# Windowed attention on one core: scores in four row groups of three heads, one division per image, values made per 128 tokens

## What is computed

```python
x = x.transpose(0, 2, 3, 1)                      # 32, 16, 16, 96
xs = roll(layernorm(x), (-4, -4))
xw = windows of 8x8 tokens                       # 128 windows, 64 tokens, 96
q, k, v = (xw @ qkv_w + qkv_b)                   # 12 heads of 8 channels; q * 8**-0.5
attn = softmax(q @ k.T + bias + mask)            # 64x64 per window and head
out = (attn @ v) @ proj_w + proj_b
x = shortcut + roll(windows back, (4, 4))
x = x + mlp(layernorm(x))
```

## Time and profile before

| | us |
|---|---|
| median of 3 runs | 540.69 |
| range of the runs | 535.23 to 543.65 |
| span of the profiled execution | 540.4 |
| TensorE busy | 518.1 (96%) |
| VectorE busy | 365.9 (68%) |
| ScalarE busy | 302.1 (56%) |
| GpSimd busy | 178.3 (33%) |

### The profile page before, as it was taken

The page is one execution under the profiler, slowest core; times in us unless marked ns, Lnnn a source line. Parts: engine busy times, 40 slices in busy tenths (PEclk is TensorE's granted clock), DMA queues, the critical chain, the costliest instruction groups (busy, mean ns, idle before and its releaser), DMA issues. The chain is left out here.

```text
span 540.4 us, 23612 instructions
## 1 busy us (share of the span) xinstructions
PE 518.1 (96%) x9134; PEld 343.1 (63%) x9134; DVE 365.9 (68%) x1003; ACT 302.1 (56%) x763; POOL 178.3 (33%) x216
## 2 busy tenths in 40 slices
PE   7999999999999999998899999939999999999996
PEld 6777777777777777776674343339655655555553
DVE  1479999999999999997404354436556565656544
ACT  2278877777787778876435563103444444444432
POOL 8433444444434443344200220022433332333300
PEclk8599999999999999999999999957999999999999
DMA  4111111111111101100130132323454434444411
GB/s 83 29 42 32 30 30 46 29 30 30 30 29 24 26 24 29 29 3 2 45 75 21 46 93 71 88 49 79 121 146 124 115 101 118 121 114 105 117 51 32
DMA packets 41177, 32.51 MB, mean 60 GB/s; under 512 B 19240, under 2 KB 36776, under 8 KB 41128
## 3 DMA queue, kind: packets, MB, share of 16 engines
q1 hardware_dynamic: 37544, 26.11, 18.9%
q0 software_dynamic: 3584, 5.72, 4.8%
HBM read 18.36 MB, written 7.13 MB: 47 GB/s over the span
## 5 line engine op out<-in xcount | busy, mean ns | idle before, releaser
L383 POOL TENSOR_TENSOR scores<-scores,peak 128x768 f32<-128x768 f32 x64 | 94.3, 1473 | 135.3 <-DVE peak L552 135.3
L1224 POOL DMA_DIRECT2D x_stack<-padded_x x96 | 52.4, 548 | 97.4 <-PE ps_v L1497 63.4
L446 ACT COPY probs_t<-ps_probs 128x768 f32<-128x768 f32 x64 | 51.1, 799 | 40.7 <-PE ps_probs L706 40.7
L544 DVE TENSOR_TENSOR scores<-ps_scores,bias 128x768 f32<-128x768 f32 x64 | 61.3, 957 | 9.1 <-PE ps_scores L696 7.4
L552 DVE TENSOR_REDUCE peak<-scores 128x12 f32<-128x768 f32 x64 | 61.0, 953 | 2.4
L719 PE MATMUL ps_out<-v_blocks,probs_t 128*64 128x54 f32 x1536 | 57.2, 224 | 1.0 <-ACT out_t L451 0.9
L719 PEld LDWEIGHTS ps_out<-v_blocks,probs_t 128*64 128x64 f32 x1536 | 50.2, 138 | 12.3 <-issue 12.2
L706 PE MATMUL ps_probs<-ident,scores 128*128 128x128 f32 x384 | 55.0, 279 | 0.0
L440 ACT ACTIVATE scores<-scores 128x768 f32<-128x768 f32 x64 | 54.2, 846 | 0.6 <-POOL scores L383 0.6
L1037 ACT ACTIVATE hidden<-ps_hidden,fc_b_folded 128x512 f32<-128x512 f32 x48 | 29.1, 688 | 36.8 <-PE ps_hidden L978 36.8
L1497 PE MATMUL ps_qk<-x_stack,conv_w 40*32 40x256 f32 x1536 | 48.8, 379 | 0.0
(11 more groups left out here) (156 smaller groups left out, 900.2 us busy)
## 6 DMA issues: line engine op xcount, KB each, us to landing
x_stack<-padded_x SPq DMA_DIRECT2D x96, 54.0 KB
x_stack<-padded_x POOLq DMA_DIRECT2D x96, 54.0 KB, 2.7
padded_x<-x_pad SPq DMA_DIRECT2D x32, 121.5 KB, 2.5
x_sliced<-stream SPq DMA_DIRECT2D x48, 64.0 KB, 2.0
mixed<-y_sliced SPq DMA_DIRECT2D x48, 64.0 KB, 2.0
out<-y_sb SPq DMA_DIRECT2D x32, 96.0 KB, 2.0
x_now<-in_x SPq DMA_DIRECT2D x32, 72.0 KB, 1.8
stream<-in_x SPq DMA_DIRECT2D x32, 72.0 KB, 1.9
```

Source lines behind the costliest of these rows:

```text
L383: nc.gpsimd.tensor_tensor(sc, sc, peak[:, par, p, :].unsqueeze(2).to_broadcast((128, HEADS, WN)), ALU.subtract).then_inc(s["shifted"], 1)
L446: nc.scalar.copy(probs_t[:, :], ps_turned).then_inc(s["turned_copied"], 1)
L544: nc.vector.tensor_tensor(scores[:, par, p, :].rearrange("p (g c) -> p g c", g=NG), ps_scores[:, :, 0:GROUP * WN], bias[:, p, :].rearrange ...
L1224: engine.dma_start(x_stack[64 * half + i * HC:64 * half + (i + 1) * HC, slot, :, :], rows).then_inc(landed[slot], 16)
```

## The change

The 12 heads are put in four row groups of three heads (24 channels, padded to 32) instead of three groups of four: the weights of queries and keys become 128 columns wide, the key copies three instead of four. Values of 128 tokens are made by one product with all 96 columns; ScalarE then moves each window's even and odd heads to the partition half where `weigh` wants them, four copies instead of two. `weigh` uses 32 columns of weights and 18 columns of values a product, four products side by side. Both halves of an image are divided at once, and both are transposed and copied in one go. The bank `ps_b` is gone: values and projection go into the tails of two banks of `ps_scores`, so `score(t, 0)` waits for the copied values and an earlier residual. `copy_v` moves forward in ScalarE's order and `make_v` and `project` move in TensorE's. The offset's folding at the start is made of 22 products (half of them with one row, adding the bias), one load fewer precedes it.

```diff
-NG = HEADS // GROUP
+TRIO = 3
+NG = HEADS // TRIO
+GROUP_C = TRIO * HD
+WIDE = 32 * NG
+PARTS_W = 4
...
-    v_blocks = sb("v_blocks", [128, 2, PAIRS, 2, HP + 2, 2, VC])
+    v_blocks = sb("v_blocks", [128, 2, PAIRS, 2, HP, 2, VC])
...
-    ps_b = bank("ps_b")
...
-    ps_v = ps_b[:, 0, 0:2 * C].rearrange("p (w q d) -> p w q d", w=2 * PAIRS, d=HD)
-    ps_proj = ps_b[0:C, 0, 0:N]
+    ps_q, ps_k = (ps_scores[:, g, N:2 * N] for g in range(2))
+    ps_v = ps_scores[:, 2, TRIO * WN:TRIO * WN + PAIRS * C].rearrange("p (a q e d) -> p a q e d", a=PAIRS, e=2, d=HD)
+    ps_proj = ps_scores[0:C, 3, N:2 * N]
...
             for e in range(2):
-                half = slice(64 * e, 64 * e + 64)
-                nc.scalar.copy(v_blocks[half, par, :, :, 0:HP, e, 0:HD].rearrange("p a b q d -> p (a b) q d"),
-                               ps_v[half]).then_inc(s["v_copied"], 1)
+                for window in range(2):
+                    nc.scalar.copy(v_blocks[64 * e:64 * e + 64, par, :, window, :, e, 0:HD],
+                                   ps_v[64 * window:64 * window + 64, :, :, e, :]).then_inc(s["v_copied"], 1)
...
-        def weigh_heads(t, p):
...
+        def weigh_heads(t):
+            dve.wait_ge(s["pv_ready"], (t + 1) * 2)
+            need(dve, s["heads_ready"], t)
+            nc.vector.reciprocal(recip[:, :, :], ps_pv[:, :, :, HD]).then_inc(s["recip_ready"], 1)
...
+            for k in range(3):
+                for g in range(NG if k < 2 else SLICES):
+                    at = k * C + g * (GROUP_C if k < 2 else 32)
+                    home = ps_biases[32 * g:32 * g + 32, k:k + 1]
+                    nc.tensor.matmul(home, w_in[:, at:at + 32], cols[:, 1:2], start=True, stop=False, skip_group_check=True)
+                    mm = nc.tensor.matmul(home, b_row[:, at:at + 32], one[:, :], start=False, stop=True, skip_group_check=True)
+                mm.then_inc(pe_set, 1)
...
         def make_v(t):
-            need(pe, s["residual_done"], t - 2)
-            heads = w_qkv[:, 2 * C:3 * C].rearrange("c (q e d) -> c q e d", e=2, d=HD)
-            for window in range(2 * PAIRS):
-                for e in range(2):
-                    mm = nc.tensor.matmul(ps_v[64 * e:64 * e + 64, window, :, :], normed[:, window * WN:(window + 1) * WN],
-                                          heads[:, :, e, :], start=True, stop=True, skip_group_check=True)
+            for p in range(PAIRS):
+                mm = nc.tensor.matmul(ps_v[:, p, :, :, :].rearrange("p q e d -> p (q e d)"), normed[:, p * 2 * WN:(p + 1) * 2 * WN],
+                                      w_qkv[:, 2 * WIDE:2 * WIDE + C], start=True, stop=True, skip_group_check=True)
...
+            if p == 0:
+                pe.wait_ge(s["v_copied"], (t + 1) * 4)
+                need(pe, s["residual_done"], t - 2)
...
-                    mm = nc.tensor.matmul(ps_scores[64 * w:64 * w + 64, g, 0:GROUP * WN], q, k, start=True, stop=True,
+                    mm = nc.tensor.matmul(ps_scores[64 * w:64 * w + 64, g, 0:TRIO * WN], q, k, start=True, stop=True,
...
-            pe.wait_ge(s["v_copied"], (t + 1) * 2)
-            need(pe, s["ot_copied"], u)
+            if p == 0:
+                need(pe, s["ot_copied"], t * PAIRS)
             pe.wait_ge(s["turned_copied"], u + 1)
             for q in range(HP):
-                for top in range(2):
-                    mm = nc.tensor.matmul(ps_out[64 * top:64 * top + 64, 0, q * 2 * VC:(q + 3) * 2 * VC],
-                                          probs_t[:, q * 128 + 64 * top:q * 128 + 64 * top + 64],
-                                          v_blocks[:, par, p, top, q:q + 3, :, :].rearrange("p q e c -> p (q e c)"),
+                for part in range(PARTS_W):
+                    at = q * 128 + 32 * part
+                    mm = nc.tensor.matmul(ps_pv[32 * part:32 * part + 32, p, 2 * q:2 * q + 2, :],
+                                          probs_t[:, at:at + 32], v_blocks[:, par, p, part // 2, q, :, :],
```

More of the change, by code:

```diff
@@ L217, in window_attention @@
     w_in = sb("w_in", [C, 3 * C])
-    w_qkv = sb("w_qkv", [C, 3 * C])
+    w_qkv = sb("w_qkv", [C, 2 * WIDE + C])
     w_proj = sb("w_proj", [C, C])
     cols = sb("cols", [C, 6])
-    b_q = sb("b_q", [C, 1])
-    b_k = sb("b_k", [C, 1])
+    b_row = sb("b_row", [1, 3 * C])
+    one = sb("one", [1, 1])
+    b_q = sb("b_q", [WIDE, 1])
+    b_k = sb("b_k", [WIDE, 1])
     b_v = sb("b_v", [C, 1])
@@ L254, in window_attention @@
     ps_folded = ps_scores[0:C, 2, 0:3 * C]
[L255 to L257 removed]
+    ps_q, ps_k = (ps_scores[:, g, N:2 * N] for g in range(2))
+    ps_v = ps_scores[:, 2, TRIO * WN:TRIO * WN + PAIRS * C].rearrange("p (a q e d) -> p a q e d", a=PAIRS, e=2, d=HD)
+    ps_proj = ps_scores[0:C, 3, N:2 * N]
     ps_turned = ps_probs.rearrange("p b c -> p (b c)")[:, 0:SC]
[L259 to L260 removed]
+    ps_pv = ps_out[:, 0, 0:PAIRS * HEADS * VC].rearrange("p (a h c) -> p a h c", h=HEADS, c=VC)
+    ps_ot = ps_out[0:C, 0, N:2 * N].rearrange("p (a n) -> p a n", a=PAIRS)
+    ps_biases = ps_out[:, 0, 0:3]
+    ps_b_proj = ps_out[0:C, 0, 3:4]
     first_homes = [ps_scores[:, 0, :], ps_scores[:, 1, :], ps_scores[:, 2, :], ps_a[:, 0, :]]
@@ L303, in _ @@
                  (cols[:, 0:1], column("L0_conv_norm1_g")), (cols[:, 1:2], column("L0_conv_norm1_b")),
-                 *((cols[:, 2 + k:3 + k], a["L0_conv_qkv_b"][k * C:(k + 1) * C].rearrange("(c a) -> c a", a=1))
-                   for k in range(3)),
-                 (head_mask[:, :], a["c_head_mask"]))
+                 (b_row[:, :], a["L0_conv_qkv_b"].rearrange("(a c) -> a c", a=1)),
+                 (head_mask[0:C, :], a["c_head_mask"][:, 0:TRIO]), (head_mask[C:WIDE, :], a["c_head_mask"][0:32, 0:TRIO]))
         second = (*((shift_mask[WN * top:WN * (top + 1), left, :], a["c_shift_mask"][WN * left:WN * (left + 1), top])
@@ L353, in _ @@
     def _(pool):
+        nc.gpsimd.memset(one[:, :], 1.0).then_inc(one_set, 1)
         nc.gpsimd.memset(eps[:, :], EPS).then_inc(zeroed, 1)
@@ L508, in set_up_projection @@
             dve.wait_ge(pe_set, 4)
-            nc.vector.tensor_tensor(b_proj[:, :], ps_out[0:C, 0, 0:1], cols[:, 5:6], ALU.add).then_inc(set_up, 1)
+            nc.vector.tensor_tensor(b_proj[:, :], ps_b_proj, cols[:, 5:6], ALU.add).then_inc(set_up, 1)
         def measure(t):
@@ L645, in fold_v @@
             pe.wait_ge(set_up, 4)
-            nc.tensor.matmul(ps_out[0:C, 0, 0:1], w_proj[:, :], b_v[:, 0:1], start=True, stop=True).then_inc(pe_set, 1)
+            nc.tensor.matmul(ps_b_proj, w_proj[:, :], b_v[:, 0:1], start=True, stop=True,
+                             skip_group_check=True).then_inc(pe_set, 1)
         def fold_mean():
@@ L781, in step @@
                 weigh(t, 1, par)
+            if real(t + 2):
+                make_v(t + 2)
+            if real(t - 1):
+                project(t - 1, 1 - par)
             if real(t + 1):
@@ L805, in step @@
                 turn_back(t + 3)
-            if real(t + 2):
-                make_v(t + 2)
             if real(t + 1):
```

107 lines of the change are left out of this document (50 added, 57 removed).

## The result

The changed kernel takes 571.24 us (median of 4 runs, 570.87 to 572.0) beside 541.54 us for the kernel before on the same chip (4 runs, 535.23 to 543.65): a ratio of 1.0633, 95% interval 1.0555 to 1.071. The direction was predicted, the size was not: 559 us was said, with 572 as the upper end of the range. Against the 540.69 us of before that is a ratio of 1.034 and an upper end of 1.058. Every ratio here leaves out the runs that fell in a slower state, so it is not the quotient of the medians beside it (571.24/541.54 is 1.055).

What follows compares the result with a forecast made beforehand. The prediction took TensorE to set the 7.05 us step, VectorE close behind. It summed 540.4 (profiled span) + 30 x 0.565 (longer steps) + 1.5 (start) = 558.9, predicting 559 us, range 538 to 572.

Steps and rivals of the forecast that it cites:

- What bounds the kernel before: Middle steps of attention: TensorE's own work sets the 7.05 us step, VectorE close behind, ScalarE third.
- The new loop through ScalarE: Middle steps: last bias addition through queries, value copies, head copies, weighing back to bias addition, 7.615 us; chance 0.62.
- Item 3: ScalarE's four value copies, 3 x 0.26 + 0.235 less an overlap of 0.10: 0.915 us.
- Item 2: TensorE's queries and keys 0.95, weighing 0.50, values 0.60, start on ScalarE 0.04: 2.09 us.
- Item 6: Lag 0.10, weighing 0.50, second-half scores 0.58, lag to VectorE 0.18, bias addition 0.96: 2.32 us.
- Items 1, 4 and 5: Bias addition to queries 0.10; logarithm to probabilities copy 1.07; that copy 0.70 plus two head copies 0.42 us.
- Start: Folding before the steps: 44 one-column products cost 2 us more, one load fewer returns 0.5, so +1.5 us.
- The second loop: VectorE through keys, division, residual, scores on shared banks, additions and measuring: 7.02 us, shorter than the first, costing nothing now.
- B: ScalarE's four value copies overlap, 0.375 us less per step, step 7.24, total 548 us; chance 0.18.
- C: Queries' wait for the last bias addition never binds; step some 6.3 us, total 519 us; chance 0.12.
- D: Floor of 33 ns per product: weighing 1.60 us, +2.2 per step, total 624 us; chance 0.03.
- E: TensorE's clock falls in attention, +2.5 us per step, some 630 us; chance 0.05.

Runs made afterwards that it cites:

- three links cut: Changed kernel with two value copies, values made ahead of the first weighing block, and second-half scores ahead of the first weighing block: 556.26 us, ratio 1.04.

## Why the prediction was right or wrong

- **What bounds the kernel before**: nearly right. TensorE is full, but the narrow weighing alone shows VectorE 0.18 us behind it. The prediction saw that it was close, and priced no gain on TensorE alone, so it cost nothing.
- **The new loop through ScalarE** is what happened, link by link and with the releasers that were named. Weighing in pairs lengthened two links by 0.27 us each, and the step grew by 0.54. The run with two value copies instead of four, the one with the deviation first and the one with the scores first each cut one link and gained 0.28 to 0.31 us. Only the copies gave nearly the full length of what was cut (0.35); for the other two the next wait took the rest.
- **The step that failed is the sum of this loop**: 7.615 us were said, and 8.10 and 7.90 in turn were measured. Two of its terms were too small. Item 3, the four value copies, was put at 0.915 and measured 1.06: an overlap of 0.10 with the next operation was taken off, and there is none (the copies end at 103.03 and the logarithm starts at 103.06); the rest is 0.27 from start to start for 0.26 and a gap of 0.03 behind the last. Item 2, queries to values, was put at 2.09 and measured 2.32 and 2.29: queries and keys 0.11 and 0.08 more, values 0.08 more, weighing 0.04 more. Item 6 is 0.03 to 0.04 more, with 0.07 too little for weighing and 0.05 too much for the lag before it. Items 1, 4 and 5 are right on the average of the two steps, and so are the lags between engines: in the longer step they are 0.15, 0.03, 0.05 and 0.19 us, together the 0.42 that the prediction put in.
- **Why queries and keys were too cheap** can be read from the runs. The prediction took their price from a kernel in which TensorE never stood. There the load of their weights starts 0.16 us ahead of the first product; after a pause load and product start within 0.04 us of each other:

```profile
104.14 0.32 PEld L672 LDWEIGHTS ps_scores<-normed,w_qkv 96*96 96x96 f32 x2
104.30 0.59 PE L672 MATMUL ps_scores<-normed,w_qkv 96*96 96x256 f32 x2
104.73 0.59 PE L674 MATMUL ps_scores<-normed,w_qkv 96*96 96x256 f32 x2
```

(before) and

```profile
99.68 0.30 PEld L684 LDWEIGHTS ps_scores<-normed,w_qkv 96*128 96x128 f32 x2 [0.38 <-DVE scores L550]
99.68 0.70 PE L684 MATMUL ps_scores<-normed,w_qkv 96*128 96x256 f32 x2
```

(changed). From queries to keys it is 0.43 us before, 0.54 and 0.50 in the changed kernel (99.68 to 100.22, 107.78 to 108.28), and again 0.45 with the same wide weights in the run with three links cut (105.13 to 105.58), where TensorE comes to the queries without a pause.
- **In us**: from image 2 to image 31 the steps cost 27.8 us more, where the sum had 17.0. These 10.8 us, with 0.65 more at the start and 1.2 less at the end, are the 10.2 us between 558.9 and the span of 569.1.
- **Start**: 1.5 said, 2.15 measured, and the closeness is partly luck. The folding takes 3.1 us more than before (4.01 for 0.88), where 2 was said, and it begins 0.86 us earlier (8.78 for 9.64), where 0.5 was said for the load. The 44 products cost 91 ns each, between the bounds, most of them at half clock. Behind it TensorE reached its full clock at 33.5 us instead of 29.4, which the prediction had nothing on.
- **Behind the steps** 1.2 us came back that the sum did not have.
- **The second loop** was said to be 7.02 us and hidden. Hidden it was; its length, once it held, is 7.43. Reciprocal and product were priced at 0.55 and take 0.78, gathering the spread was left out (0.15), and the keys were put 0.17 too short.
- **Rivals.** B: four copies in 1.03 us, not 0.65. C: TensorE waits for the bias addition in every step read of the changed kernel. D: weighing in 0.54 us, not 1.60. The Trainium skill (TensorEngine Tiling (Array Packing), Performance Considerations, Instruction Overhead) gives some 60 cycles for each of these small products, an estimate of 25 ns at 2.4 GHz; the trace has 11 ns, so it does not hold for four products side by side, while for two side by side 18 moving columns cost as much as 54, which is the rule's sense. E: the granted clock is 1.00 from 40 to 240 us although TensorE is busy 173.7 of these 200 us only.

## What to carry to other kernels

When a change moves an operation into a queue or lets two results share a bank, write the loop that it closes as a list of links. Price each link as it runs behind a pause, and take no overlap off that was not seen for this very pair of operations: here prices from a kernel in which nothing waited came out 5% short (7.615 for 7.99). Then look for the next longest loop, and the one after that, before pricing a repair; here the next lay 0.3 us below the first and another 0.6 below, and cutting three links of the first won only these 0.6 us. A change of many parts is worth taking apart: the narrow weighing and the single division, in an order that fits them, make the kernel 1 to 2% faster (ratios 0.9881 and 0.9818). Of the rest, the four copies cost 0.30 us a step and the place of the second scores 0.31. With three links cut the step is still 7.39 us, and VectorE stands 0.91 us of it for scores whose bank the residual has just left; that the shared banks are what remains is the reading of these waits and was not run by itself.

## What the runs showed of the hardware

- Weighing with 64 columns of weights, two side by side, costs 34 ns a product (an instruction of the record) with 18 as with 54 moving columns; with 32 columns of weights, four side by side, 11 ns. The width of the weights and the number side by side change together here; the moving columns, from 18 to 54, did not matter.
- The four value copies on ScalarE, each on 64 partitions, start 0.27 us apart at a length of 0.24: they do not overlap each other, nor the operation behind them (logarithm, or the copy of the probabilities in the run with the deviation first), while the scaling ahead of them in that run does (99.12 + 0.57 = 99.69, the first copy starts at 99.58). Only two of the four move data to the other partition half, and the two copies of the kernel before, which stay in their half, do not overlap either. What all the pairs without overlap share is that input or output begins at another partition than in the operation before; the scaling and the first copy both begin at partition 0. No run changed this alone.
- The first product behind a pause of TensorE takes longer to the next: 0.50 to 0.54 us for the queries' product of 256 columns, 0.43 to 0.46 without a pause.
- Products of 96 rows and of one row in turn, with one moving column, cost 0.15 us each (two instructions) at full clock (8.78 to 8.93), and 0.19 to 0.20 from 9.7 us on, where the granted clock is 0.50.
- The spread of the kernel before, 532.28 to 544.05 us in eleven runs on one chip, goes with the mean granted clock of the run, 0.983 and 0.962 at these two. The run with two value copies does not follow this: 561.95 us at 0.966 and 562.98 at 0.985. TensorE reached its full clock at 29.4 us in the profile before, at 33.5 in the changed kernel, and at 13.9 in the one with the narrow weighing alone, whose start has the same folding and filling as that of before; ahead of the rise it had been busy 20.13 of 20.40, 24.38 of 24.50 and 4.90 of 4.90 us. What decides this was not found, and it moves a single run by more than the whole start of the change.
